# Inverse roots of variances cut into pieces of two or three operations over sixteen tiles, and four rounding rests spread over four steps

## The reference, cut to what matters

```python
x = x + _L0_attn_ref(_layernorm(x, axis=-1), wq, wk, wv, wo)             # 16 heads, window of 256
x = x + _L0_xattn_ref(_layernorm(x, axis=-1), ctx_2048, ctx_2048, gamma)  # 8 heads over features
x = x + _L0_ffn_ref(_layernorm(x, axis=-1), router_w, router_b, expert_w, expert_b)
```

```python
def _L0_xattn_ref(q, k, v, gamma):
    ...
    qk = jnp.einsum('bhdq,bhdl->bhql', qh, kh) * scale
    sm = jax.nn.softmax(qk, axis=-1)
    ret = jnp.einsum('bhql,bhdl->bhdq', sm, vh)
```

## Time and profile before

| | |
|---|---|
| median of 3 runs | 2607.47 us |
| the profiled execution, its own time | 2608.79 us |
| its span, first to last instruction | 2607.0 us |
| busy: PE, DVE, ACT, POOL | 2510.3, 1891.8, 961.1, 857.1 us |
| mean granted TensorE clock | 0.986 of full |

### The profile page before, as it was taken

How to read it: one execution, slowest core, us unless ns; L and a number is a source line. 1 busy time by engine, 2 the same in 40 slices (tenths; PEclk the granted TensorE clock), 3 DMA queues, 4 the chain that set the end, 5 groups by cost and what they waited for, 6 DMA issues and landing times.

```text
span 2607.0 us, 36672 instructions
## 1 busy us (share of the span) xinstructions
PE 2510.3 (96%) x12428; PEld 1884.6 (72%) x12428; DVE 1891.8 (73%) x3996; ACT 961.1 (37%) x2441; POOL 857.1 (33%) x692
## 2 busy tenths in 40 slices
PE   7999999999999999999999999999989999998996
PEld 5788888888888888888888888888734444443674
DVE  7878887666667667666766677777778888887657
ACT  3332233322222232222223222222347777776321
POOL 3211111421111132111213211112348888887200
PEclk9999999999999999999999999999989999999998
DMA  3222323321122232112323211122356666663003
GB/s 121 65 94 97 121 94 114 102 77 65 65 97 98 81 101 78 65 65 82 106 89 102 77 65 65 65 97 106 134 174 203 220 213 217 220 217 117 5 1 129
DMA packets 170198, 280.56 MB, mean 108 GB/s; under 512 B 15136, under 2 KB 81696, under 8 KB 170016
## 3 DMA queue, kind: packets, MB, share of 16 engines
q1 hardware_dynamic: 170016, 278.23, 31.8%
HBM read 185.37 MB, written 92.27 MB: 106 GB/s over the span
## 4 chain that ended last, share of the span: by engine, by line
PE 87%; DVE 4%; SPq 3%; DMA 3%; issue 1%; ACT 1%; POOL 1%; DVEq 0%; ACTq 0%; POOLq 0%
PE pj L669 26%; PE pj L690 14%; PE pj L666 13%; PE ob L720 4%; PE sc L701 4%; PE pj L745 4%; PE ob L756 3%; PE tr L709 3%; PE sc L734 3%; DMA qst<-xmlo 2%; PE sc L700 2%; PE ob L721 2%; PE pj L768 2%; PE tr L734 1%; PE pj L908 1%
## 5 line engine op out<-in xcount | busy, mean ns | idle before, releaser
L669 PE MATMUL pj<-xnt,whi 128*128 128x512 f32 x2048 | 717.4, 412 | 6.6 <-issue 4.5
L958 ACT ACTIVATE pr<-sc,nmx 128x128 f32<-128x128 f32 (+1 forms) x512 | 210.6, 416 | 996.5 <-DVE nmx L1187 996.4
L535 POOL TENSOR_TENSOR qt<-rot,swp 128x512 f32<-128x512 f32 x128 | 165.9, 1296 | 1025.7 <-DVE swp L1163 1025.7
L669 PEld LDWEIGHTS pj<-xnt,whi 128*128 128x128 f32 x2048 | 386.9, 189 | 87.5 <-issue 5.4
L669 PE MATMUL pj<-xnt,wlo 128*128 128x512 f32 x1024 | 399.8, 390 | 0.0
L666 PE MATMUL pj<-whi,xnt 128*128 128x512 f32 x1024 | 357.4, 410 | 1.4 <-issue 1.4
L561 POOL TENSOR_TENSOR xprt<-xprt,xprt 128x512 f32<-128x512 f32 x256 | 320.6, 1284 | 90.3 <-PE ob L756 90.3
L1015 ACT ACTIVATE xprt<-pj 128x512 f32<-128x512 f32 x512 | 290.8, 595 | 142.0 <-PE pj L745 140.5
L1161 DVE TENSOR_TENSOR rot<-pj,trig 128x512 f32<-128x512 f32 x256 | 176.6, 690 | 139.6 <-PE pj L669 138.5
L1277 DVE TENSOR_REDUCE xnmx<-sc 128x1 f32<-128x512 f32 x342 | 227.7, 682 | 64.4 <-PE sc L734 64.3
L535 POOL TENSOR_TENSOR kt<-rot,swp 128x512 f32<-128x512 f32 x128 | 164.9, 1288 | 300.8 <-DVE swp L1163 300.8
(11 more groups left out here) (193 smaller groups left out, 4288.1 us busy)
## 6 DMA issues: line engine op xcount, KB each, us to landing
xnt<-xt_scratch SPq DMA_DIRECT2D x48, 1024.0 KB, 9.7
x_scratch<-xio SPq DMA_DIRECT2D x64, 512.0 KB, 3.5
xio<-x_scratch SPq DMA_DIRECT2D x48, 512.0 KB, 4.1
qst<-sq_scratch SPq DMA_DIRECT2D x192, 128.0 KB, 2.6
kst<-sk_scratch SPq DMA_DIRECT2D x192, 128.0 KB, 2.6
raw<-in_w_all_dram SPq DMA_DIRECT2D x64, 256.0 KB, 3.1
xt_scratch<-xnt SPq DMA_DIRECT2D x16, 1024.0 KB, 8.2
sq_scratch<-qp SPq DMA_DIRECT2D x32, 512.0 KB, 3.4
```

Of the source, the lines that this page charges most:

```text
L535: nc.gpsimd.tensor_tensor(qk["QK".index(kind)][h][:, :, :].rearrange("p b n -> p (b n)"), rot[r % 2][:, :], swp[r % 2][:, :], ALU.add).the ...
L669: last = nc.tensor.matmul(bank[:, :], wpart[:, w, i * HD:(i + 1) * HD], moving, start=(k == 0), stop=(k == 3 * CB - 1))
L958: nc.scalar.activation(pr[:, a % 4, lo:hi], SC[a % 2][:, lo:hi], ACT.Exp, bias=nmx[:, a % 4, t:t + 1], accum_out=rsum[:, a % 4, t:t + 1]). ...
```

## The change

`roots` and `y_roots` are cut into a seed (3 operations), a turn (3) and, for the cross stage, the scales (2). DVE's program has these pieces in other places; what each operation computes is the same.

- The other sixteen tiles' roots of the cross stage: seed at the end of the step with c = 1 of tile 2, a turn at the same place of tiles 3, 4, 5 and 6, the scales at that of tile 7. They are first used for tile 16.
- The mix's roots: seed for tiles 0 to 15 at that place of tile 22, turns at tiles 23 to 26; tiles 16 to 31 in the joined steps 8 (seed) to 12.
- `y_normed(1)` stands at the end of step 123, one step later than `y_normed(0)`.
- One `expert_rest` in each of the steps 129 to 132, for two in 129 and 130.

```diff
@@ -1255,15 +1256,18 @@
                 ins.then_inc(c_step, 1)
                 dve.wait_ge(c_step, x_steps[0])
 
-            def roots(t):
+            def x_seeds(t):
                 x_step(nc.vector.tensor_scalar(var2[:, t], mv2[:, t, 1], EPS, None, ALU.add))
                 x_step(nc.vector.tensor_scalar(seed2[:, t], var2[:, t].bitcast(I32), 1, None, ALU.logical_shift_right))
                 x_step(nc.vector.tensor_scalar(rstd2[:, t].bitcast(I32), seed2[:, t], -1.0, float(0x5f3759df),
                                                ALU.mult, ALU.add))
-                for _ in range(4):
-                    x_step(nc.vector.scalar_tensor_tensor(half2[:, t], rstd2[:, t], -0.5, rstd2[:, t], ALU.mult, ALU.mult))
-                    x_step(nc.vector.tensor_tensor(half2[:, t], half2[:, t], var2[:, t], ALU.mult))
-                    x_step(nc.vector.scalar_tensor_tensor(rstd2[:, t], half2[:, t], 1.5, rstd2[:, t], ALU.add, ALU.mult))
+
+            def x_turn(t):
+                x_step(nc.vector.scalar_tensor_tensor(half2[:, t], rstd2[:, t], -0.5, rstd2[:, t], ALU.mult, ALU.mult))
+                x_step(nc.vector.tensor_tensor(half2[:, t], half2[:, t], var2[:, t], ALU.mult))
+                x_step(nc.vector.scalar_tensor_tensor(rstd2[:, t], half2[:, t], 1.5, rstd2[:, t], ALU.add, ALU.mult))
+
+            def x_scales(t):
                 x_step(nc.vector.tensor_scalar(rstd2[:, t], rstd2[:, t], XSCALE, None, ALU.mult))
                 nc.vector.scalar_tensor_tensor(shift2[:, t], mv2[:, t, 0], -1.0, rstd2[:, t],
                                                ALU.mult, ALU.mult).then_inc(c_shift, 1)
@@ -1314,14 +1318,15 @@
                 ins.then_inc(f_rs, 1)
                 dve.wait_ge(f_rs, y_steps[0])
 
-            def y_roots(t):
+            def y_seeds(t):
                 y_step(nc.vector.tensor_scalar(y_var[:, t], mv3[:, t, 1], EPS, None, ALU.add))
                 y_step(nc.vector.tensor_scalar(y_seed[:, t], y_var[:, t].bitcast(I32), 1, None, ALU.logical_shift_right))
                 y_step(nc.vector.tensor_scalar(y_rstd[:, t].bitcast(I32), y_seed[:, t], -1.0, float(0x5f3759df), ALU.mult, ALU.add))
-                for k in range(4):
-                    y_step(nc.vector.scalar_tensor_tensor(y_half[:, t], y_rstd[:, t], -0.5, y_rstd[:, t], ALU.mult, ALU.mult))
-                    y_step(nc.vector.tensor_tensor(y_half[:, t], y_half[:, t], y_var[:, t], ALU.mult))
-                    y_step(nc.vector.scalar_tensor_tensor(y_rstd[:, t], y_half[:, t], 1.5, y_rstd[:, t], ALU.add, ALU.mult))
+
+            def y_turn(t):
+                y_step(nc.vector.scalar_tensor_tensor(y_half[:, t], y_rstd[:, t], -0.5, y_rstd[:, t], ALU.mult, ALU.mult))
+                y_step(nc.vector.tensor_tensor(y_half[:, t], y_half[:, t], y_var[:, t], ALU.mult))
+                y_step(nc.vector.scalar_tensor_tensor(y_rstd[:, t], y_half[:, t], 1.5, y_rstd[:, t], ALU.add, ALU.mult))
 
             def y_normed(n):
                 if n == 0:
@@ -1378,6 +1383,11 @@
                     y_normed(n + 2)
                 if n < TILES:
                     y_rest(n)
+                if n == JOIN:
+                    dve.wait_ge(c_bn, 2 * TILES)
+                    y_seeds(LAST_HALF)
+                if JOIN < n <= JOIN + 4:
+                    y_turn(LAST_HALF)
                 if n == JOIN:
                     dve.wait_ge(f_ebhi, 1)
                     nc.vector.tensor_tensor(y_ebp[XD:XD + 1, :], y_eb[XD:XD + 1, :], y_ebp[XD:XD + 1, :].bitcast(F32),
@@ -1434,7 +1444,10 @@
                         k_first_rest(*part)
                 if s == TAIL - 30:
                     dve.wait_ge(s_bn, 2 * ROOTS)
-                    roots(slice(0, ROOTS))
+                    x_seeds(FIRST_HALF)
+                    for _ in range(4):
+                        x_turn(FIRST_HALF)
+                    x_scales(FIRST_HALF)
                 for k in range(*SCORES_AT.get(s - TAIL, (0, 0))):
                     maximum(k // 4, k % 4)
                 if s == TAIL + MAX_AT + 1:
@@ -1442,30 +1455,35 @@
             dve.wait_ge(s_bn, 2 * TILES)
             for s in range(X_LAST):
                 n, c = s // CB, s % CB
-                if s == 2 * CB:
-                    roots(slice(ROOTS, TILES))
                 for q in range(XPT):
                     if s + AHEAD < X_STEPS:
                         maximum(s + AHEAD, q)
                     for do, d in X_WORK.get((c, q), ()):
                         if tile(n + d):
                             do(n + d)
+                if c == 1 and n == 2:
+                    x_seeds(LAST_HALF)
+                if c == 1 and 2 < n <= 6:
+                    x_turn(LAST_HALF)
+                if c == 1 and n == 7:
+                    x_scales(LAST_HALF)
+                if c == 1 and n == ROOTS + 6:
+                    dve.wait_ge(c_bn, 2 * ROOTS)
+                    y_seeds(FIRST_HALF)
+                if c == 1 and ROOTS + 6 < n <= ROOTS + 10:
+                    y_turn(FIRST_HALF)
                 if s == X_STEPS - CB - 2:
-                    dve.wait_ge(c_bn, 2 * (TILES - CB))
-                    y_roots(slice(0, TILES - CB))
                     y_normed(0)
+                if s == X_STEPS - CB - 1:
                     y_normed(1)
                 if s == X_STEPS - CB:
                     dve.wait_ge(f_rwhi, 1)
                     nc.vector.tensor_tensor(y_rwp[1][:, :, 0:E], y_rw[:, :, :], y_rwp[0][:, :, 0:E].bitcast(F32),
                                             ALU.subtract).then_inc(f_rwlo, 1)
-                if s in (X_STEPS + 1, X_STEPS + 2):
-                    for c in range(2 * (s - X_STEPS - 1), 2 * (s - X_STEPS)):
-                        expert_rest(c)
+                if X_STEPS < s <= X_STEPS + CB:
+                    expert_rest(s - X_STEPS - 1)
                 if joined(s) is not None:
                     joined_step(joined(s))
-            dve.wait_ge(c_bn, 2 * TILES)
-            y_roots(slice(TILES - CB, TILES))
             for n in range(JOIN, TILES + 3):
                 joined_step(n)
             dve.wait_ge(f_pt, 1)
```

More of the change, by code:

```diff
@@ L314, in decoder_stages @@
         ROOTS = TILES // 2
+        FIRST_HALF, LAST_HALF = slice(0, ROOTS), slice(ROOTS, TILES)
         ov = out.rearrange("b (t p) d -> b p t d", p=P)
```

## The result

The changed kernel takes 2620.33 us in the median of 5 runs (2614.96 to 2623.04), beside 2607.47 us for the kernel before in 5 runs (2606.66 to 2608.67). The ratio is 1.0045, 95% interval [1.0033, 1.0057]: slower by 12.9 us, where the prediction had +9.5. The five runs differ in TensorE's mean granted clock: 0.988 at 2614.96 and 0.987 at 2616.01, but 0.984, 0.985 and 0.984 in the three slower ones.

What follows compares the result with a forecast made beforehand. PE was taken as nearly full, stopped twice by DVE's roots. Stops and expert rests -16.9, pieces, scales and absorbed waits +17.3, clock +9.1: +9.5 us, about 2617 us; range 2600 to 2626, forecast's own 2610 to 2621.

Steps and rivals of the forecast that it cites:

- The mechanism: Cross stage: root operations inside POOL's bursts each end with an addition, delaying the next maximum; PE waits 2.0 us per piece.
- The two stops: PE's waits behind DVE's roots at tile 2 and at tiles 30 and 31 vanish: -8.3 and -7.4 us.
- Late `y_normed(1)`: End of step 123: if held behind a POOL addition, it makes `output` late, costing up to 1 us.
- The pieces: Ten seeds and turns in tiles 2 to 6 and 22 to 26 cost PE 2.0 us each, +20.0 us.
- the scales: Tile 7: two operations end late enough to make PE wait, +0.7 us.
- What the waits for the transfer absorb: At the ten pieces, a later PE skips some waits for the maxima's transfer: -3.4 us, other bound 0.
- The clock: TensorE's clock falls behind seven of the ten 2 us waits, 1.3 us each: +9.1 us, bounds 0 and +13.
- The expert rests: Joined steps: two rests instead of four before `y_rest` shorten PE's wait, later two cost nothing: -1.2 us.
- Hidden: Rival: turns under 1.5 us stay within DVE's cover, PE never waits, both stops go: 2590.6 us; chance 0.18.
- Held, clock stays: Rival: pieces are held by POOL but TensorE's clock falls rarely or never: about 2608 us; chance 0.18.
- worse: Rival: the clock falls at every piece and late `max_rest` delays the transfer in ten tiles: about 2625 us; chance 0.08.

Runs made afterwards that it cites:

- experiment 1: The changed kernel with all root pieces at the end of steps with c = 1 moved to their start: 2595.52 us, ratio 0.9949 to the kernel before.
- experiment 6: The kernel before with three spare chained two-input operations at the start of the step with c = 1, tiles 9 to 20: 2609.52 us, ratio 0.9997.
- experiment 5: The kernel before with three spare chained two-input operations at the end of the step with c = 1, tiles 9 to 20: 2663.17 us, ratio 1.0196.
- experiment 2: The changed kernel with root pieces at the start of steps with c = 1 and expert rests two per step again: 2594.55 us, ratio 0.9942.
- experiment 4: The changed kernel with two root operations per place instead of three, end of steps with c = 1, tiles 2-10 and 20-27: 2598.32 us, ratio 0.9961.
- experiment 3: The kernel before with only the expert rests changed, one in each of steps 129 to 132: 2608.00 us, ratio 0.9997.
- experiment 7: The kernel before with three spare chained one-input reductions at the end of the step with c = 1, tiles 9 to 20: 2611.20 us, ratio 1.0000.

## Why the prediction came out right, and where it did not

The median of 2620.33 lies in the forecast's own range (2610 to 2621), near its end: +12.9 us for +9.5 said. In the traced execution, from the first weigh to the last, +9.2 us stand against +10.7 said (the sum without the expert rests). Most terms hit singly, as shown below. That the total is near is partly luck: the falls of the clock, nearly all of the forecast's +9.5, cost 6.2 us in the trace for 9.1 said, and what they cost in the slower executions, where the median lies, no trace shows.

*The mechanism was right in each step.* Each root operation in a burst of POOL ends with an addition (1.00, 1.20, 1.19 us for 0.9, 1.2, 1.2 said), the third at the burst's end. The maximum behind it is the one that PE wants, and PE waits. Experiments 1 and 6 take POOL's additions away from the operations and the cost is gone; experiment 5 puts the cost into tiles that the change leaves alone.

*The two stops*: -8.28 and -7.43, said -8.3 and -7.4. *Late `y_normed(1)`*: up to 1 us feared, nothing seen. The `sums` of 2414.70 has no wait; the 0.2 us for `output` in the list of waits is that of the last tile, where the kernel before has it as well (0.24).

*The pieces*: 2.07 each, said 2.0; the scales 0.70, said 0.7. In twos 0.86.

*What the waits for the transfer absorb*: said -3.4 with 0 as the other bound. Behind the ten pieces of the changed kernel PE waits for the transfer of maxima not once, and in the kernel before five times in these tiles, 3.5 us together. Behind the twelve pieces of experiment 5 there is no such wait either. So the -3.4 was right, and that `max_rest` is late as well did no harm. The ledger shows only -1.04 since it holds all tiles, and the slow weighs behind three falls (1.6 us). In the tiles without a piece these waits vary among executions: the steps from part 3 to part 0's weigh are 4.0 us longer in experiment 1, which holds nothing, than before, and PE's waits for the transfer between 1960 and 2300 us were 6.8 us before, 6.3 after, 10.2 and 11.9 in experiments 1 and 2, 5.2 in experiment 4.

*The clock*: said seven falls of ten at 1.3 us, +9.1, bounds 0 and +13. The profiled execution had four of ten, at tiles 2, 5, 22 and 26. They cost 1.60, 0.89, 1.24 and 0.86 us in the step itself (7.91, 7.20, 7.55 and 7.19 from weigh to weigh, less 4.24 and 2.07, the fourth from 4.26), and in three of them the next weigh is slow as well, 0.3 to 0.7 us: 4.6 + 1.6 = 6.2 together, 1.6 each, so fewer falls than said, each a little dearer. The runs of 2620 to 2623 us had a mean clock lower by 0.003 to 0.004, which fits more falls there; how many of the ten fell in them no trace shows. Experiment 5 shows that the upper bound was too low: a fall can cost 2.2 us in its step, and 0.8 in the next, where the ten of the prediction were bounded at 1.3 each.

*The expert rests*: said -1.2, and no gain seen. This is the step that failed, though a small one. Its first half was right: the first wait is 1.2 us shorter (2.90 to 1.70 in experiment 3). Its second half, that the later two rests cost nothing, was not: waits of about the same size come behind them. The times alone would not refute the term, as the interval of experiment 3 holds -1.2. I had followed only the `y_rest` behind the rests, and took the later two for free because "PE has logits to do". The logits themselves wait: ACT's evacuation of the first takes all four rests, and what is queued on DVE behind the fourth, which POOL holds, is the next `y_rest`. I had not asked who waits for the moved instruction, only who stands behind it.

*The rivals.* Hidden: its point of decision, a turn under 1.5 us, was the right one; experiment 1 is this rival made true. There the forecast was 2590.6 and 2595.5 was measured, 13.3 us under before and not 16.9: 1.2 of the difference are the expert rests, whose gain is not there; the rest, 2.4, is within the scatter of the transfer's waits and of the falls behind them (+4.0 in its trace). "Held, clock stays" fell with the four falls; "worse" was not reached in the median.

## What to carry to other kernels

Before work is cut up to fill an engine's idle share, look at what the neighbour that can hold it up does at the very place: here the same 32 instructions cost 25 us more at one place than at another, some 3 us away in the same step. A piece is free while its time, as held, stays under the lead that the engine has over its reader (three banks, about 1.5 us here by the prediction's estimate; a hold of 3.46 us left a wait of 1.80); one operation too many costs PE's wait, and beyond some length the clock too. For a moved instruction ask both who stands behind it and who waits for its result, and count the two as separate terms.

## What the runs showed of the hardware that I had not expected

- Equal waits, unequal clocks. A wait of 1.80 us at the same matmul was followed by the lower clock in 4 of 10 cases in the changed kernel, and in 11 of 12 in experiment 5, the last ten in a row, one in each tile (20.5 us). The lower level began right behind the wait in the ten (0.80 us for the first matmul, 0.50 in the changed kernel), and 0.8 to 1.7 us later in the four. The waits for the transfer of maxima are as mixed: in the traces of experiments 1, 2, 3 and 7 those of 1.25, 1.35, 1.64, 1.64, 1.68 and 1.74 us were followed by it, those of 1.30, 1.41 and 1.48 us not. Waits of 0.6 us for a maximum were never followed by it (15 waits in experiment 4). What decides between them the runs don't settle.
- POOL pays nothing for a hold: its bursts of four take 4.98 to 4.99 us with three held operations (22 bursts) and 4.96 to 5.04 without, while DVE gets one through per addition, at 1.19 us for 0.17.
- A reduction that reads SBUF passes through the same burst at 0.17 us. An operation that must stand there could be given one input elsewhere; that was not tried.
